# A graph network's first pass: how VectorE makes the weighted and the plain one-hots

## The reference, cut to what matters

```
L0:  msg  = relu(h[src] + edge_attr_16 @ We + be)
     aggr = segment_sum(msg, dst)                  # then a small MLP
L1:  deg_out, deg_in = sums of w by src, by dst    # with one loop edge per node
     wn   = w * rsqrt(deg_out)[src] * rsqrt(deg_in)[dst]
     10 times: h = 0.9 * segment_sum(h[src] * wn, dst) + 0.1 * h0
L2:  three layers of attention over edges, L3: an edge convolution
```

## Time and profile before

| | |
|---|---|
| median of 3 runs | 5595.54 us (5579.65 to 5604.3) |
| profiled execution, span | 5635.3 us (the profile gives no other time of this execution) |
| mean granted PE clock | 0.781 of full speed |
| before the first pass | 0 to 713 us |
| first pass (L0 and the dense matrix) | 713 to 1516 us |
| L0's end and L1's ten steps | 1516 to 2300 us |
| three passes of L2, one of L3 | 2300 to 5635 us |
| busy in the span | PE 3433.8, POOL 3082.6, DVE 2812.2, ACT 928.0 us |

### The profile page before, as it was taken

The page is one execution under the profiler, slowest core; times in us unless marked ns, Lnnn a source line. Parts: engine busy times, 40 slices in busy tenths (PEclk is TensorE's granted clock), DMA queues, the critical chain, the costliest instruction groups (busy, mean ns, idle before and its releaser), DMA issues.

```text
span 5635.3 us, 80038 instructions
## 1 busy us (share of the span) xinstructions
PE 3433.8 (61%) x20001; PEld 2425.2 (43%) x20012; DVE 2812.2 (50%) x10008; ACT 928.0 (16%) x3266; POOL 3082.6 (55%) x3058
## 2 busy tenths in 40 slices
PE   2440078878889999656656556666566666344444
PEld 2330034444433444355556455555455556233333
DVE  7840088878621111355555455555555556533333
ACT  0000023333200000011112111112111112111111
POOL 3787676656688880145555345555255554355544
PEclk9999999989899999777777577777677777555555
DMA  4311123323599999411111211112111112011101
GB/s 139 82 26 9 47 67 74 83 70 80 133 331 344 356 352 356 165 40 43 42 43 42 38 41 43 42 43 41 38 43 43 42 43 40 18 20 19 19 18 21
DMA packets 293594, 498.20 MB, mean 88 GB/s; under 512 B 169174, under 2 KB 207203, under 8 KB 291962
## 3 DMA queue, kind: packets, MB, share of 16 engines
q1 hardware_dynamic: 118407, 339.94, 17.0%
q0 software_dynamic: 92160, 115.72, 11.2%
q10 hardware_dynamic: 82800, 40.01, 2.5%
HBM read 435.57 MB, written 58.97 MB: 88 GB/s over the span
## 4 chain that ended last, share of the span: by engine, by line
PE 38%; another core or an unknown queue 21%; DVE 14%; issue 13%; POOL 8%; ACT 2%; DMA 1%; DVEq 1%; ACTq 1%; SPq 0%; POOLq 0%
PE ps L1502 34%; POOL rows_dst L755 8%; DVE arena L1103 3%; DVE arena L1102 2%; PE ps L1728 2%; DVE arena L1121 1%; DVE arena L1119 1%; PE ps L1605 1%; DVE arena L1117 1%; DMA arena<-in_edge_attr_dram 1%; PE ps L1680 1%; DVE arena L1275 1%; ACT arena L1468 1%; DVE arena L1280 1%
## 5 line engine op out<-in xcount | busy, mean ns | idle before, releaser
L770 POOL DMA_INDIRECT arena<-table,arena x2080 | 2085.0, 1002 | 2200.4 <-DMA arena<-rows_dst 1299.9
L1502 PE MATMUL ps<-arena 128*128 128x96 f32 (+3 forms) x9176 | 1605.9, 354 | 573.3 <-issue 174.3
L1502 PEld LDWEIGHTS ps<-arena 128*128 128x128 f32 (+3 forms) x9176 | 1138.9, 207 | 953.3 <-issue 623.6
L1605 PE MATMUL ps<-ident,arena 128*96 128x128 f32 x416 | 149.9, 360 | 1123.1 <-ACT arena L1468 570.6
L1102 DVE TENSOR_SCALAR arena<-iota_row_b,arena 128x128 bf16<-128x128 bf16 x1664 | 438.3, 264 | 695.4 <-remote 518.6
L1502 PE MATMUL ps<-arena,nodes 125*64 125x500 f32 (+2 forms) x3144 | 649.6, 538 | 27.2 <-DVEq L1194 16.5
L755 POOL DMA_INDIRECT rows_dst<-stage,arena x400 | 483.7, 1209 | 196.3 <-issue 121.6
L1103 DVE TENSOR_SCALAR arena<-iota_row_b,arena 128x128 f32<-128x128 bf16 x2080 | 582.5, 298 | 0.0
L1605 PEld LDWEIGHTS ps<-ident,arena 128*96 128x96 f32 x416 | 65.3, 157 | 1190.5 <-ACT arena L1468 588.3
L1115 DVE TENSOR_TENSOR arena<-ps,arena 128x256 f32<-128x256 f32 x416 | 175.4, 422 | 787.3 <-remote 614.9
L728 POOL DMA_INDIRECT rows_src<-stage,stage_at x400 | 485.1, 1213 | 118.5 <-issue 116.6
(11 more groups left out here) (284 smaller groups left out, 3858.7 us busy)
## 6 DMA issues: line engine op xcount, KB each, us to landing
arena<-dense SPq DMA_DIRECT2D x240, 750.0 KB
nodes<-dense SPq DMA_DIRECT2D x60, 750.0 KB
dense<-arena ACTq DMA_DIRECT2D x150, 250.0 KB
arena<-table,arena POOLq DMA_INDIRECT x2080
arena<-dense SPq DMA_DIRECT2D x60, 500.0 KB
arena<-rows_dst SPq DMA_DIRECT2D x208, 96.0 KB
arena<-dense SPq DMA_DIRECT2D x6, 2000.0 KB
arena<-pair_rows SPq DMA_DIRECT2D x12, 976.6 KB
```

Of the source, the lines that this page charges most:

```text
L770: nc.gpsimd.indirect_dma_start(rows[:, u, k, 0:width], None, frm, bass.IndirectOffsetOnAxis(ap=p[:, c, j, c_other:c_other + 1].bitcast(I32 ...
L1502: return nc.tensor.matmul(to, lhsT, rhs, start=start, stop=stop, skip_group_check=True)
L1605: nc.tensor.transpose(to, pay[:, c, j:j + K, :].rearrange("p k c -> p (k c)"), ident[:]).then_inc(tr_ready, 1)
```

## The change

In `dense_operands` every step now makes its three weighted one-hots by the scalar-tensor-tensor that odd steps had. In `one_hots` the branch without the turned copy, which only the first pass takes, makes the unit's four one-hots by one comparison of two tensors: the row 0 to 127, broadcast over the four tiles, against the four keys, each broadcast over 128 columns (128 x 512, f32 out). The branch of the later passes stays as it was.

```diff
@@ dense_operands
                     v.wait_ge(built, i * PER_BODY + (first + k + 1))
-                    if (first + k) % 2:
-                        nc.vector.scalar_tensor_tensor(
-                            lhs[:, slot], iota_row_b[:].unsqueeze(1).to_broadcast([128, 3, 128]), lo_col[:, bass.ds(tile_at, 1)],
-                            w_parts[:, bass.ds(tile_at, 1), :].rearrange("p o c -> p (o c)").unsqueeze(2).to_broadcast([128, 3, 128]),
-                            ALU.is_equal, ALU.mult)
-                    else:
-                        for part in range(3):
-                            nc.vector.tensor_scalar(lhs[:, slot, part, :], iota_row_b[:], lo_col[:, bass.ds(tile_at, 1)],
-                                                    w_left[:, part, bass.ds(tile_at, 1)], ALU.is_equal, ALU.mult)
+                    nc.vector.scalar_tensor_tensor(
+                        lhs[:, slot], iota_row_b[:].unsqueeze(1).to_broadcast([128, 3, 128]), lo_col[:, bass.ds(tile_at, 1)],
+                        w_parts[:, bass.ds(tile_at, 1), :].rearrange("p o c -> p (o c)").unsqueeze(2).to_broadcast([128, 3, 128]),
+                        ALU.is_equal, ALU.mult)
                     nc.vector.tensor_scalar(rhs[:, slot, :], iota_col_h[:], flat_keys[:, bass.ds(key_at, 1)], None,
                                             ALU.is_equal).then_inc(op_ready, 1)
@@ one_hots
                 if weights:
                     nc.vector.tensor_copy(of(msg, v_)[:, :, D], p[:, c, j0:j0 + K, C_W])
+                if not turned:
+                    nc.vector.tensor_tensor(of(oh, v_), iota_row_b[:].unsqueeze(1).to_broadcast([128, K, 128]),
+                                            p[:, c, j0:j0 + K, c_key].unsqueeze(2).to_broadcast([128, K, 128]),
+                                            ALU.is_equal).then_inc(oh_ready, 1)
+                    return
                 for k in range(K):
                     key_at = p[:, c, j0 + k, c_key:c_key + 1]
-                    if turned:
-                        nc.vector.tensor_scalar(of(ohb, v_)[:, k, :], iota_row_b[:], key_at, None, ALU.is_equal)
+                    nc.vector.tensor_scalar(of(ohb, v_)[:, k, :], iota_row_b[:], key_at, None, ALU.is_equal)
                     ins = nc.vector.tensor_scalar(of(oh, v_)[:, k, :], iota_row_b[:], key_at, None, ALU.is_equal)
                 ins.then_inc(oh_ready, 1)
```

## The result

The changed kernel takes 5654.8 us (median of 4 runs, 5637.2 to 5668.1) against 5596.8 of the kernel before (4 runs, 5579.7 to 5604.3): ratio 1.0117, 95% interval [1.0084, 1.0149]. It is slower by about 58 us. The forecast was 5576, in a range of 5538 to 5606: wrong, and on the wrong side of no change.

The account below looks back on a forecast made before the run. PE was taken to set the first pass's pace, with ACT's clears, its unit boundaries and its clock. Of 61 us less DVE work 20 were on the path: 5595.5 - 20 = 5575.5, say 5576, range 5538 to 5606.

Parts of the forecast that it names:

- DVE is relieved of 61 us: First pass: dense steps save 43 us of DVE time and one-hots 18 us, 61 in all (5 to 115).
- Only some 20 us of it are on the path: First pass: DVE's saving counts only in PE's 20 waits for its operands, 1.0 us each, 20 us.
- fall towards 12 us: Sign to look for: PE's waits for DVE's L1087 in the first pass fall from 30.9 towards 12 us.
- DVE sets the pace: Rival: DVE paces the first pass, so nearly all 61 us are gained, 5538 us; chance 0.20.
- nothing moves: Rival: PE is held by ACT and its clock, so the time stays at 5588 to 5600 us; chance 0.20.
- The loop boundary: DVE's 4.79 us idle start of a loop turn stays; counted as zero, at most 1 us x 11.
- Other queues: No DMA, wait or semaphore is added; POOL's 168 us of waiting for tables hides a gather that grows a little.
- The third rival: DVE's two-tensor instructions lengthen POOL's gathers; decides past 1.63 us each, 52 us more at 1.75, 5648 us; chance 0.10.

Follow-up runs that it names:

- e6: The changed kernel with one gather a unit instead of four in the first pass; pass 681 us, ratio to before 0.9821.
- e5: The kernel before with one gather a unit instead of four in the first pass; pass 696 us, ratio to before 0.9844.
- e13: The changed kernel with one extra one-column tensor-scalar in every dense step and three at each unit's one-hots; ratio to before 1.0245.
- e7: The kernel before with three short tensor-scalars in every dense step and one gather a unit in the first pass; ratio to before 0.9871.
- e16: The changed kernel with gathers of 16 columns instead of 64 in the first pass, as many gathers; pass 832 us, ratio to before 1.0100.
- e17: The changed kernel run once more, unaltered; pass 856 us, ratio to before 1.0110.
- e1: The changed kernel with the old four tensor-scalars for the one-hots put back, so only the dense steps are changed; ratio to before 1.0174.
- e2: The kernel before with only the one-hots changed to one 512-column comparison, dense steps still alternating; ratio to before 1.0064.
- e4: The changed kernel with two extra one-column tensor-scalars at each even dense step and three at each unit's one-hots; ratio to before 0.9959.
- e18: The padded changed kernel (e4) run once more; pass 746 us, ratio to before 0.9945.
- e9: The kernel before with a GpSimd memset and a wait for it ahead of each first-pass gather; pass 912 us, ratio to before 1.0171.
- e10: The changed kernel with two extra one-column tensor-scalars at each even dense step and none at the one-hots; ratio to before 1.0012.
- e3: The kernel before with three short tensor-scalars in every dense step and no long one, old one-hots; pass 880 us, ratio to before 1.0155.
- e14: The changed kernel with three extra one-column tensor-scalars at each unit's one-hots alone; pass 872 us, ratio to before 1.0199.
- e15: The changed kernel with two extra one-column tensor-scalars in every dense step and three at each unit's one-hots; ratio to before 1.0170.
- e8: The changed kernel with a GpSimd memset and a wait for it ahead of each first-pass gather; pass 952 us, ratio to before 1.0278.
- e11: The changed kernel with three one-column GpSimd memsets ahead of each gather, waited for once in eight gathers; ratio to before 1.0140.

## Why the prediction was wrong, step by step

- **DVE is relieved of 61 us.** Right: 57 (655.7 to 598.5). The comparison takes 684 ns (0.69 taken).
- **Only some 20 us of it are on the path.** Not shown. With few gathers, e6's pass is 15 us shorter than e5's, but the runs don't tell the two apart, and PE's waits for DVE's operands, where the gain was put, are 24.1 us in e6 and 22.4 in e5. After the change they don't fall towards 12 us, but are 53.8. That DVE sets the pace and that nothing moves, the first two rivals, are out: the kernel is slower by 58 us.
- **The loop boundary.** Nothing hung on it, and the rows don't answer it. The waits before DVE's L1098 that end in "issue" fell from 47.0 us to 19.2, but all waits at that place rose from 72 to 120 us. Before, and then after:

```profile
DVE arena L1098 <- PE ps L1502: 14.5, 15, 5.6
DVE arena L1098 <- remote: 10.8, 4, 3.0
```

```profile
DVE arena L1093 <- PE ps L1501: 35.2, 37, 8.8
```

- **Other queues.** This is the step that failed. It read the gather's 1199 ns as the whole of the matter between DVE and POOL, saw 168 us in which POOL waits for its tables, and costed a longer gather at nothing. As far as it goes that was true: PE waits 6.9 us for gathered rows after the change. But the price of a gather isn't paid by whoever waits for its rows. The kernel before already paid 103 us for three gathers in four, by increments of PE that come late, standstills, slow register instructions and the lower clock that goes with them (0.92, against 0.98 in e5); the changed one pays 176. No row quoted shows that directly; the "remote" waits (163 us before, 19.9 of them in the earlier trace rows) and the bodies of 71 and 74 us at clocks of 0.86 and 0.82 were its traces, and I put them down to PE and its clock without asking what stopped PE.
- **The third rival**, the gathers, had the right side, the right engines and a time (5648) near the result, at a chance of 0.10, by another mechanism: that is luck. It was to decide when a gather passes 1.63 us, because POOL would then be late. The mean is 1.37, and POOL isn't late. e13 comes nearest to that rival (1.78 us, PE waits 42 us for rows), with shut-outs and late increments besides.

**What is shown and what isn't.** Shown: the loss comes with the gathers (e5 to e7); it lies in the instruction and its rows more than in bytes (e16); while gathers run close behind one another, increments of PE arrive late and DVE, ACT and then PE stand for them (130 late before, 165 to 172 in after, e17, e1 and e2, 38 and 13 in e4 and e18, at most 5 in e5 to e9), and so it is with the slow register instructions of PE and DVE (none in e5 to e9); removing the short instructions of the even steps brings shut-outs (0 to 24; back to 1 or 2 with pads in pairs and at the one-hots, to 17 with the pairs at even steps alone).

Only argued: that shut-outs cause the quick runs after them, as at 931 to 964, and that the length of the runs is what matters. For it: unbroken runs of six or more gathers, each started under 1.35 us behind the last, number 0 in e18, 2 in before and e4, 5 in e2, 7 in e10, 14 in after and e17, 16 in e1, 19 in e3, nearly in the order of the passes; this gives e2 its place too, which has no shut-out and only 10 more quick gathers than before. Against it: e14 has 10 and a pass of 872 us (e13 and e15 are held by POOL and DVE). e3 has such runs without a shut-out, by never holding a gather back at all. In part quick gathers are also the effect, since a DVE that stands doesn't hold POOL.

Open: through what a run of gathers holds up the increments of PE and the registers of three engines.

## What to carry to other kernels

Where GpSimd issues gathers beside a busy VectorE, take away most of the gathers in a copy of the kernel before you price a change of VectorE: it tells in one run what the gathers cost, and here that was more than any edit was worth. Don't judge a gather by its mean or by who waits for its rows; look for gathers several times the usual length, for unbroken runs of the shortest ones, for stretches in which all engines but GpSimd stand, and there for a consumer that starts long after its producer ended. Replacing short instructions by a long one can close the gaps in which GpSimd worked, and a version with useless short instructions in pairs can be the quicker one, as e4 and e18 were here.

## What the runs showed of the hardware that was not expected

- A gather that meets alternating 384-column two-tensor and 500-column one-tensor instructions takes up to 6.10 us in the changed kernel; while DVE stands (958 to 964 us) a gather takes 0.95.
- In unbroken runs of quick gathers, increments of PE arrive up to 20.2 us late, in order, while those of DVE arrive within 0.01 us in the changed kernel; PE, DVE and ACT can all stand for 8 us (958.4 to 966.5).
- In the same runs, single register instructions of PE, DVE and ACT take about 0.70 us.
- A wait of GpSimd for its own memset costs 0.78 us behind the memset's 0.31 (e8); three one-column memsets without a wait fit in the 0.30 us between two gathers (e11).
- A one-column tensor-scalar of DVE with a per-partition scalar takes 264 to 279 ns (the pads of e4, e13, e15 and e18).
